# Normalisation of x moved from VectorE to ScalarE, and the value products regrouped, in the attention prologue

## The reference, cut to what matters

```python
def _layernorm(x, axis=-1, eps=1e-05):
    m = jnp.mean(x, axis=axis, keepdims=True)
    v = jnp.var(x, axis=axis, keepdims=True)
    return (x - m) / jnp.sqrt(v + eps)
...
x = x + jnp.tanh(g_ffn[0]) * _L0_ffn_ref(_layernorm(x, axis=-1), ...)
x = x + jnp.tanh(g_xattn[1]) * _L1_xattn_ref(_layernorm(x, axis=-1), ctx_4096, ctx_4096, mask, wq, wk, wv, wo, 0)
...
q = (query @ wq)   # 1024 x 512 by 512 x 4096, then rotary embedding
k = (key @ wk)     # 1024 x 512 by 512 x 1024, then rotary embedding
v = (value @ wv)   # 1024 x 512 by 512 x 1024
```

## Time and profile before

| what | us |
|---|---|
| median of 3 runs (lowest to highest) | 804.2 (802.8 to 807.0) |
| the profiled execution's own time | 806.3 |
| its span, from the first to the last instruction | 804.5 |
| PE busy (share of the span) | 762.8 (95%) |
| DVE busy | 640.2 (80%) |
| POOL busy | 388.6 (48%) |
| ACT busy | 352.2 (44%) |
| start of the second attention's first value products | 178.06 |
| start of the first score of the loop | 216.21 |

### The profile page before, as it was taken

How to read it: one execution, slowest core, us unless ns; L and a number is a source line. 1 busy time by engine, 2 the same in 40 slices (tenths; PEclk the granted TensorE clock), 3 DMA queues, 4 the chain that set the end, 5 groups by cost and what they waited for, 6 DMA issues and landing times.

```text
span 804.5 us, 12801 instructions
## 1 busy us (share of the span) xinstructions
PE 762.8 (95%) x4278; PEld 607.7 (76%) x4278; DVE 640.2 (80%) x1209; ACT 352.2 (44%) x1077; POOL 388.6 (48%) x352
## 2 busy tenths in 40 slices
PE   3899998898989999999999999999999999999996
PEld 2576675887767778888878888877888888787875
DVE  5999997879888787767878777787877778868985
ACT  2878884412333423343342334334333433344664
POOL 2889986415553533323353333335333333386784
PEclk9899999998999999999999999999999999999998
DMA  8310140100021111011111100111110012210011
GB/s 258 104 53 26 33 124 2 40 28 25 29 63 42 52 39 42 26 32 40 35 46 38 51 27 27 40 40 41 39 54 27 27 34 85 56 30 1 2 40 66
DMA packets 37463, 37.45 MB, mean 47 GB/s; under 512 B 2912, under 2 KB 27232, under 8 KB 37408
## 3 DMA queue, kind: packets, MB, share of 16 engines
q1 hardware_dynamic: 35488, 33.20, 13.8%
q10 hardware_dynamic: 1920, 3.54, 1.4%
HBM read 34.64 MB, written 2.10 MB: 46 GB/s over the span
## 4 chain that ended last, share of the span: by engine, by line
PE 62%; DVE 8%; POOL 5%; issue 2%; ACT 1%; POOLq 0%; DVEq 0%; ACTq 0%
PE ROW L2080 6%; PE QB L2082 6%; PE QB L2080 6%; PE QB L2081 6%; PE SB L2195 6%; PE ROW L2081 6%; PE ROW L2082 6%; PE PB L2168 4%; DVE rope_b L1695 2%; PE KV L719 2%; PE KV L2080 2%; PE TB L2138 2%; PE KV L2082 1%; PE KV L2081 1%; PE KV L720 1%
## 5 line engine op out<-in xcount | busy, mean ns | idle before, releaser
L1260 POOL TENSOR_TENSOR dense<-rope_a,rope_b 128x512 f32<-128x512 f32 x62 | 79.2, 1278 | 163.8 <-DVE rope_b L1695 163.8
L1474 ACT ACTIVATE ot_hi<-PB 128x512 fp32r<-128x512 f32 x64 | 38.3, 598 | 199.2 <-PE PB L2168 199.1
L1463 ACT ACTIVATE e_sb<-masked,nmax 128x64 f32<-128x64 f32 x256 | 86.1, 337 | 57.0 <-DVE nmax L1726 56.7
L2080 PE MATMUL QB<-xT_hi,wq_lo 128*128 128x512 f32 x256 | 106.9, 417 | 0.0
L2080 PE MATMUL ROW<-wo_hi,ot_lo 128*128 128x512 f32 x256 | 102.1, 399 | 0.8 <-DVE ot_lo L1754 0.8
L2082 PE MATMUL QB<-xT_hi,wq_hi 128*128 128x512 f32 x256 | 101.7, 397 | 0.0
L2081 PE MATMUL QB<-xT_lo,wq_hi 128*128 128x512 f32 x256 | 101.6, 397 | 0.0
L1692 DVE TENSOR_TENSOR rope_a<-QB,rope 128x512 f32<-128x512 f32 x62 | 42.8, 691 | 73.9 <-PE QB L2082 71.8
L2081 PE MATMUL ROW<-wo_lo,ot_hi 128*128 128x512 f32 x256 | 101.6, 397 | 0.0
L2082 PE MATMUL ROW<-wo_hi,ot_hi 128*128 128x512 f32 x256 | 101.1, 395 | 0.0
L1695 DVE TENSOR_TENSOR rope_b<-QB,rope 64x512 f32<-64x512 f32 x124 | 85.4, 688 | 3.9
(11 more groups left out here) (215 smaller groups left out, 1883.4 us busy)
## 6 DMA issues: line engine op xcount, KB each, us to landing
raw<-in_wq SPq DMA_DIRECT2D x32, 256.0 KB, 2.7
raw<-in_wo SPq DMA_DIRECT2D x32, 256.0 KB, 2.6
ctx_two<-in_ctx SPq DMA_DIRECT2D x16, 256.0 KB, 3.8
x_sb<-in_x SPq DMA_DIRECT2D x8, 256.0 KB, 6.8
ctx_raw<-in_ctxT ACTq DMA_DIRECT2D x1, 2048.0 KB, 12.6
raw<-in_wv SPq DMA_DIRECT2D x8, 256.0 KB, 2.7
raw<-in_wk SPq DMA_DIRECT2D x8, 256.0 KB, 2.8
out<-x_sb SPq DMA_DIRECT2D x8, 256.0 KB, 2.0
```

The costliest lines, as they stand in the source:

```text
L1260: nc.gpsimd.tensor_tensor(dst, a, b, ALU.add).then_inc(s_rot, 1)
L1463: nc.scalar.activation(e_sb[:, r, :], masked[:, r, :], ACT.Exp, bias=nmax[:, r:r + 1], accum_out=zsum[:, r:r + 1]).then_inc(s_exp, 1)
L1474: nc.scalar.activation(ot_hi[:, :, :].rearrange("p h (b q) -> p b h q", b=2), PB2[:, :, 0:256].rearrange("p b (h q) -> p b h q", h=GH), AC ...
L2080: nc.tensor.matmul(out, lhs[1], rhs[0], start=first, stop=False)
```

## The change

VectorE no longer normalises. It computes a row shift, -mean * rstd, for four tiles at once (`row_shift`, one small instruction of 128x4), and ScalarE writes scale * x + shift with an Identity activation. The value products 5 and 6 move ahead of the transposes of tiles 0 to 3, so that 2 to 6 run in one go, and value 7 moves from behind the last query to between the transposes of tiles 1 and 2. ScalarE's and VectorE's orders follow. The instructions of the loop stay as they are.

```diff
+            def normalize_x(t):
+                act.wait_ge(s_shift, 1 + t // 4)
+                nc.scalar.activation(dense[:, t, :], x_sb[:, t, :], ACT.Identity, bias=shift[:, t:t + 1],
+                                     scale=rstd[:, t, :]).then_inc(s_xn, 1)
...
-            def normalize_x(t):
-                nc.vector.tensor_scalar(dense[:, t, :], x_sb[:, t, :], mv[:, t, 0:1], rstd[:, t, :],
-                                        ALU.subtract, ALU.mult).then_inc(s_xn, 1)
+            def row_shift(a, b):
+                nc.vector.scalar_tensor_tensor(out=shift[:, a:b], in0=mv[:, a:b, 0], scalar=-1.0,
+                                               in1=rstd[:, a:b, 0], op0=ALU.mult, op1=ALU.mult)\
+                  .then_inc(s_shift, 1)
...
-            for tile in (2, 3, 4):
+            for tile in range(2, 7):
                 pe.wait_ge(s_vlo, tile - 1)
                 value(tile, FIRST_V[tile])
-            for t in range(4):
+            for t in range(2):
                 transpose_x(t)
-            for tile in (5, 6):
-                pe.wait_ge(s_vlo, tile - 1)
-                value(tile, FIRST_V[tile])
+            pe.wait_ge(s_vlo, 6)
+            value(7, FIRST_V[7])
+            for t in range(2, 4):
+                transpose_x(t)
             pe.wait_ge(s_xlo, 4)
```

More of the change, by code:

```diff
@@ L1142, in attention_and_swiglu @@
         c = c | {"wo": wo}
+        shift = sb("shift", [P, TILES])
+        s_shift = sem("row_shift_ready")
         magic = sb("magic", [P, 1])
@@ L1486, in round_x @@
                                      ACT.Copy).then_inc(s_xhi, 1)
+            def normalize_x(t):
+                act.wait_ge(s_shift, 1 + t // 4)
+                nc.scalar.activation(dense[:, t, :], x_sb[:, t, :], ACT.Identity, bias=shift[:, t:t + 1],
+                                     scale=rstd[:, t, :]).then_inc(s_xn, 1)
             for tile in range(5):
                 round_v(0, tile, FIRST_V[tile])
-            for t in range(TILES):
+            normalize_x(0)
+            round_v(0, 5, FIRST_V[5])
+            normalize_x(1)
+            round_x(0)
+            normalize_x(2)
+            round_v(0, 6, FIRST_V[6])
+            round_x(1)
+            normalize_x(3)
+            round_x(2)
+            round_v(0, 7, FIRST_V[7])
+            round_x(3)
+            for t in range(4, TILES):
+                normalize_x(t)
+            for t in range(4, TILES):
                 round_x(t)
-                if t in (3, 4):
-                    round_v(0, t + 2, FIRST_V[t + 2])
-            round_v(0, 7, FIRST_V[7])
             for place in range(FIRST, len(NEXT)):
@@ L1796, in _ @@
             gate_linear(7)
+            rest_v(0, 3, FIRST_V[3])
             dve.wait_ge(s_rstd, 1)
-            for t in range(4):
[L1799 to L1805, removed]
+            row_shift(0, 4)
+            rest_v(0, 4, FIRST_V[4])
+            rows(5)
+            rest_v(0, 5, FIRST_V[5])
+            rest_x(0)
+            rows(6)
+            rest_v(0, 6, FIRST_V[6])
+            rest_x(1)
+            rows(7)
             dve.wait_ge(s_mv, TILES)
             variance_eps(nc, c, s_var, 4, TILES)
+            rest_x(2)
+            rest_v(0, 7, FIRST_V[7])
+            rest_x(3)
             dve.wait_ge(s_tab, 48)
             dve.wait_ge(s_rstd, 2)
-            for t in range(4, TILES):
-                normalize_x(t)
+            row_shift(4, TILES)
             for h in range(GH):
@@ L1814, in _ @@
                 rest_x(4 + h)
-                if h < 2:
-                    rest_v(0, 5 + h, FIRST_V[5 + h])
                 if h == 1:
                     rope_first(q_job(0, h - GH) + 1, s_k, 1, KV, 1)
-            rest_v(0, 7, FIRST_V[7])
             def pair(gp, ahead):
@@ L2126, in _ @@
                 transpose_x(4 + h)
-            pe.wait_ge(s_vlo, 6)
-            value(7, FIRST_V[7])
             pe.wait_ge(s_parts, 3 * (q_job(0, 1 - GH) + 1) + 3)
```

## The result

The changed kernel takes 806.53 us in the median (802.71 to 811.59, 22 runs), the kernel before beside it 804.98 (802.80 to 807.00, 22 runs). The ratio is 1.0027 with a 95% interval of 1.0014 to 1.0040: slower by about a quarter of a per cent, inside the 0.5% that the prediction called no change. Timed again later it gave 1.0024 (1.0005 to 1.0044), with 806.40 against 803.94 us.

The account below looks back on a forecast made before the run. The prediction took the prologue's path to TensorE's first score as the bound; VectorE's freed 5.75 us yield to ScalarE, the value products and a longer queue, so 804.2 + 1.3 = 805.5 us, range 802.5 to 808.5.

Parts of the forecast that it names:

- The bound: Prologue: TensorE is busy 95% of the span, so edits outside the loop count only by moving the score at 216.21 us.
- ScalarE's normalisations: ScalarE in the prologue: eight Identity activations at 0.81 us each, with no blocking by GpSimd.
- The shift: VectorE's two 128x4 shifts: between nothing and 0.68 us each, covered, so adding nothing to the sum.
- Values 5 and 6, and the transposes of tile 0: TensorE: transposes start at 193.2 us with a short clock spell, 194.4 with a long one; middle 193.8 taken.
- VectorE's queue to query 0: VectorE's low parts and row statistics ahead of query 0 take 4.9 us, so it starts at 200.05, 2.6 us later.
- ScalarE just in time for this queue: Tiles 2 and 3 rounded by about 199 us, wanted at 198.4 and 199.3; VectorE waits for roundings behind normalisations.
- From query 0 to the score: Rotary parts to score: 14.72 us less 0.68 plus a 0.45 wait for query 1; score at 217.54, 1.3 us later.
- The price of query 0: Query 0's start to the first rotary part: 2.95 us plus 0.05, from 200.05 to 203.05.
- a short spell over the queries: Rival: a 3.4 us half-clock spell after the gap before query 0 costs 1.7 us, giving 807.2 us; chance 24%.
- The sum: Whole kernel: +1.3 us, giving 805.5 us; +0.7 and +1.9 by the other ends of values 5 and 6; 48%.
- The test that the prediction named: Score later than 219 with the clock at 0.50 between 199 and 206 would show a spell over the queries.
- All of VectorE's 5.75 us comes off: Rival: VectorE's work alone sets the score, so 5.4 us come off after the shifts, giving 798.8 us; chance 4%.

Follow-up runs that it names:

- b: Changed kernel's orders on all engines, but VectorE normalises again at the two places of the shifts; 808.74 us, ratio 1.0056 to the kernel before.
- a: Kernel before with only the normalisation moved to ScalarE, the old orders kept; 804.76 us, ratio 1.0003 to the kernel before.
- c: Changed kernel with VectorE's row statistics of tiles 6 and 7 and the epsilon moved up; 804.81 us, ratio 1.0007 to the kernel before.
- e: Changed kernel with eight unused products on TensorE in the gap before query 0; 804.28 us, ratio 1.0000 to the kernel before.
- a2: Like a, but ScalarE does two of its last four normalisations before rounding tile 4 and two behind it; 805.24 us, ratio 0.9997 to before.
- f: Changed kernel reordered: values 2 to 5, four transposes, value 6, queries, value 7; statistics before low parts of x; 802.83 us, ratio 0.9975 to before.
- g: Like e, plus seven more unused products on TensorE before the wait of value 4; 803.96 us, ratio 1.0001 to the kernel before.

## Why the prediction was right, point by point

- *The bound.* Right. Time outside the loop counted only as far as it moved the first score; between before and after the rest behind the score stayed within 0.21 us.
- *ScalarE's normalisations*, 0.80 to 0.82 us: 797 to 817 ns, the first one beside GpSimd's additions too. Right. b and a show by experiment that they are not what costs.
- *The shift*, bounded between nothing and 0.68 us. Outside its bound: 0.92 us in the changed kernel and 1.25 in a for the first, 0.15 for the second. It was covered all the same, because tile 0 was ready at 190.43 (189.61 + 0.82) and TensorE came to it at 194.08.
- *Values 5 and 6, and the transposes of tile 0.* Right at both ends. From the first value product, the prediction's 194.4 and 193.2 are 16.3 and 15.1; the profiles have 16.40 with the long spell and 14.96 with the short one. The middle that the forecast used was in none of them.
- *VectorE's queue to query 0.* 195.60 to 200.61 is 5.01 us, against 4.9 in the sum; the same 5.01 in the second course. Right.
- *ScalarE just in time for this queue.* Too strict, and so is the sentence that a rounding behind a normalisation makes VectorE wait. Behind tile 0 the roundings were ready early: that of tile 3 at 198.47 + 0.60 = 199.07, and VectorE came to it at 199.88. It waited for none of tiles 1 to 3. Only in c, with the statistics out of the way, did it wait for ScalarE there, 0.28 and 0.49 us.

```profile
198.47 0.60 ACT L1486 ACTIVATE xT_hi<-ROW 128x512 fp32r<-128x512 f32 x1
```

- *From query 0 to the score.* First rotary part to score: 219.79 - 205.27 = 14.52, against 14.72 - 0.68 + 0.45 = 14.49. Right, the new wait for query 1 (0.36 us) included.
- *The price of query 0*, 3.0 us from its start to the first rotary part. This is the mis-sized term: 3.10 us at full clock, but 205.27 - 200.61 = 4.66 in the profiled execution. The prediction had this as its rival of a short spell over the queries, at +1.7 us for an execution that has it, and 24% against 48%. It is no alternative to the forecast but a part of it: one kernel shows both courses, and the forecast itself has no term for the spell.
- *The sum.* +0.7 for the short first spell: measured 38.87 - 38.15 = 0.72 where no spell lay over the queries, and 0.69 in e. For the long one, +1.9 and +1.7 make +3.6; measured +3.96. The medians moved by 1.55 us (806.53 - 804.98) against the +1.3 of the forecast. That these two lie so close is in part luck: no profile shows +1.3, and the median stands between executions near +0.7 and executions near +4.0. The test that the prediction named, score later than 219 with the clock at 0.50 between 199 and 206, was met by the first profile to the letter; in the second, counted from the first value product of before, the score stands at 178.06 + 38.87 = 216.93, inside the 216.9 to 218.1 of the forecast.
- *All of VectorE's 5.75 us comes off*: refuted. Even a, with its orders unchanged, gained 0.26 us at the score.

What stays open: how often the spell falls over query 0. Two of the three profiles of the changed kernel had it, and the gap was the same in all three (2.18, 2.17 and 2.17 us). What decides it in a single execution is not shown. That it is the empty gap which makes it possible is supported by e, where nothing else was changed and no run was long, and by c, which shortens the gap; both also show no spell over query 0 in their two profiles each. It is not shown beyond these counts.

## What to carry to other kernels

Taking work off the engine that stands on the critical path is worth only the distance to the next engine in line: here three other orders with ScalarE's normalising gave -0.26 (a), -0.25 (a2) and -1.80 or -2.57 us (f) at the score, and in a and a2 the waits in VectorE's timeline name the queue that gave the gain back. When regrouping leaves TensorE a gap of some two microseconds ahead of a long product, price the gap and the half clock behind it, and look whether rows or products can be moved into it. Compare prologues from a common event, not from the span's start, and read more than one profile before a difference of a microsecond is believed.

## What the runs showed of the hardware that was not expected

- A 128x4 instruction on VectorE with two inputs in SBUF took 0.92 us (after) and 1.25 us (a) beside GpSimd's addition, and 0.15 and 0.16 us when GpSimd was idle. GpSimd's rows in the profile after, and its additions in that of a, where the shift began at 186.35:

```profile
187.04 3.76 POOL L1256 TENSOR_TENSOR x_sb<-x_sb,dense 128x512 f32<-128x512 f32 x3
199.12 1.01 POOL L63 TENSOR_TENSOR rstd<-veps,mhalf 128x4 f32<-128x4 f32 x1 [8.32 <-DVE veps L57]
...
185.08 3.73 POOL L1256 TENSOR_TENSOR x_sb<-x_sb,dense 128x512 f32<-128x512 f32 x3
```

  In the profile after the three additions run from 187.04 to 190.80, across the first shift at 188.66 and not the second at 200.47. The Trainium skill, page "SBUF — State Buffer", section "Who interferes with whom", says that VectorE's second port pair is shared with GpSimd under an exclusive lock. The trace fits that; the numbers add that an instruction of four columns can wait some 0.8 to 1.1 us for it, so its size is no measure of its price there.
- The granted clock fell over query 0 after gaps of 2.18 and 2.17 us without work on TensorE in two profiles, and not after one of 2.17 in a third. It did not fall there after gaps of 1.48 and 1.49 us (c), nor of 0.32 and 0.34 (e). The length of the gap alone does not tell. A gap of 1.74 to 1.77 us ahead of value 4 stands in thirteen of the fourteen profiles (g fills it); the clock fell within 1.5 us behind it in eleven and did not in a2 and in the first profile of f. Behind the gap of 1.66 to 1.70 us ahead of the score it fell in five of the nine profiles that have it.
- Products that nobody needs, put into such a gap, did not make query 0 later (21.19 and 21.18 us against 21.24), and the kernel with them took 0.23% less time (e against after in one timing, 0.9977, 0.9957 to 0.9997); part of that can lie at the kernel's end, as said above.
